# Moving a speculative check's branch and a first product, and re-dealing the splitting of weights between two engines

## The reference

```
h = W.T[x]                                  # one embedding row per token
a = layernorm(h)
s_t = tanh(A s_(t-1) + B a_t)               # a recurrence over 512 positions, s_0 = 0
o = C s
h = h + Wo (sigmoid(Wg o + bg) * o) + bo
f = layernorm(h)
e = argmax(gate_w f)                        # one of 8 experts for each token
h = h + w2[e] (silu(w1[e] f) * (w3[e] f)) + sw2 gelu(sw1 f)
```

## Time and profile before

| | |
|---|---|
| median of 3 runs | 182.56 us (180.62, 182.56, 183.18) |
| profiled execution | 182.58 us, of which the span from first to last instruction 180.7 us |
| mean granted TensorE clock | 0.971 of 2.4 GHz |
| busy: PE, DVE, ACT, POOL | 77%, 70%, 58%, 47% of the span |
| steps 15 to 53 of the recurrence | about 33 to 70 us from the span's start |
| pipeline over pairs, choice of experts | 70 to 99 us |
| gathers and blocks of tokens | 99 to 181 us |

### The profile page before, as it was taken

The page is one execution under the profiler, slowest core; times in us unless marked ns, Lnnn a source line. Parts: engine busy times, 40 slices in busy tenths (PEclk is TensorE's granted clock), DMA queues, the critical chain, the costliest instruction groups (busy, mean ns, idle before and its releaser), DMA issues.

```text
span 180.7 us, 3231 instructions
## 1 busy us (share of the span) xinstructions
PE 138.5 (77%) x997; PEld 99.7 (55%) x997; DVE 127.2 (70%) x365; ACT 104.7 (58%) x239; POOL 84.1 (47%) x77
## 2 busy tenths in 40 slices
PE   0105997788898888886799988899939989999720
PEld 0104864666675666675445878466726657666510
DVE  1245676927499995999779899488825778887730
ACT  2001444589989983587779993675532645655400
POOL 3768874900000000343100658552687787886580
PEclk9999999969999999999999999999996999999995
DMA  4564345899000000012200033410122443433331
GB/s 153 150 184 138 97 140 195 278 384 365 7 0 0 4 0 4 2 60 95 79 4 0 29 91 114 134 32 16 47 45 31 45 42 33 44 33 34 29 33 15
DMA packets 9955, 14.37 MB, mean 80 GB/s; under 512 B 1936, under 2 KB 4624, under 8 KB 9936
## 3 DMA queue, kind: packets, MB, share of 16 engines
q1 hardware_dynamic: 5904, 10.45, 16.9%
q0 software_dynamic: 4032, 3.67, 13.3%
HBM read 10.71 MB, written 3.41 MB: 78 GB/s over the span
## 4 chain that ended last, share of the span: by engine, by line
DMA 22%; PE 20%; POOL 18%; DVE 14%; ACT 12%; issue 10%; POOLq 1%; SPq 1%; DVEq 0%
DMA w_sb<-x_rows,row_in 7%; PE bank L655 6%; POOL w_sb L415 6%; POOL emb_rows L371 5%; DMA emb_rows<-emb,tok_sb 5%; POOL out L422 4%; PE bank L680 4%; DMA xblk<-x_rows,row_in 4%; ACT attn_out L725 4%; DMA w_sb<-w 3%; ACT states L702 3%; ACT w_hl L742 3%; PE bank L478 2%; PE bank L668 2%; DMA out<-w_sb,row_of 2%
## 5 line engine op out<-in xcount | busy, mean ns | idle before, releaser
L422 POOL DMA_INDIRECT out<-w_sb,row_of x20 | 31.3, 1564 | 9.1 <-DVE w_sb L1205 4.8
L478 PE MATMUL bank<-states,sq_sb 128*128 128x128 f32 x108 | 27.1, 335 | 6.0 <-ACT states L702 1.6
L655 PE MATMUL bank<-w_hl,xblk_t 128*128 x120 | 30.4, 391 | 1.0 <-issue 1.0
L403 POOL TENSOR_TENSOR rstd<-vareps,cst 128x2 f32<-128x2 f32 x8 | 5.7, 710 | 45.7 <-DVE vareps L853 45.7
L478 PEld LDWEIGHTS bank<-states,sq_sb 128*128 128x128 f32 x108 | 17.4, 202 | 14.2 <-ACT states L702 13.8
L812 ACT ACTIVATE w_sb<-bank,factor 128x512 f32<-128x512 f32 x20 | 13.8, 688 | 19.4 <-PE bank L655 19.3
L476 PE MATMUL bank<-x_in,sq_sb 128*128 128x128 f32 x108 | 23.3, 299 | 1.6 <-ACT x_in L695 1.5
L415 POOL DMA_INDIRECT w_sb<-x_rows,row_in x16 | 17.5, 1094 | 12.4 <-issue 6.3
L702 ACT ACTIVATE states<-bank 128x128 f32<-128x128 f32 x54 | 14.9, 276 | 12.2 <-PE bank L478 12.0
L680 PE MATMUL bank<-w_hl,w_sb 128*128 x160 | 16.6, 246 | 5.7 <-DVE w_sb L1205 5.7
L476 PEld LDWEIGHTS bank<-x_in,sq_sb 128*128 128x128 f32 x108 | 17.9, 207 | 2.8 <-ACT x_in L695 1.6
(11 more groups left out here) (160 smaller groups left out, 288.9 us busy)
## 6 DMA issues: line engine op xcount, KB each, us to landing
w_sb<-w SPq DMA_DIRECT2D x24, 256.0 KB, 6.4
x_rows<-norm SPq DMA_DIRECT2D x4, 256.0 KB, 2.4
out<-attn_out SPq DMA_DIRECT2D x4, 256.0 KB, 3.1
late<-places SPq DMA_DIRECT2D x1, 619.5 KB, 8.3
sw_sb<-sw SPq DMA_DIRECT2D x2, 256.0 KB, 3.0
cst<-consts SPq DMA_DIRECT2D x1, 420.0 KB, 3.3
sq_sb<-sq SPq DMA_DIRECT2D x1, 384.0 KB, 3.7
out<-w_sb,row_of POOLq DMA_INDIRECT x20, 3.3
```

Source lines behind the costliest of these rows:

```text
L422: pool.indirect_dma_start(out=out, out_offset=bass.IndirectOffsetOnAxis(ap=row_of[:, k:k + 1], axis=0), in_=out_blk[k % RING], in_offset=N ...
L478: pe.matmul(pre, at, states[:, i * COLS:(i + 1) * COLS], start=False, stop=True).then_inc(pre_ready, 1)
L655: mm = pe.matmul(hb[:], xblk_t[:, k % 3, b * P:(b + 1) * P], w[:, bass.ds(e * INNER + a * EXPERTS * INNER, INNER)], start=(j == 0), stop=( ...
```

## The change

(1) `gate(0)` goes from behind step 51 to behind step 49, and the product with C of pair 0 from behind the branch to behind step 50, into bank 6 in place of bank 0. (2) The branch comes behind step 51 in place of step 52, with `gate(1)` ahead of it; steps 52 and 53 both come behind the branch. VectorE's `gated` of pair 0 waits for a new semaphore that TensorE raises behind the branch. (3) The first three experts' low halves of w1 are written ahead of the wait for the squares, in one instruction; the fourth takes the place of the third between the two waits for TensorE. (4) The four last high halves of w2 are written by VectorE in one instruction, not by ScalarE behind steps 48 to 51, and their low halves in one instruction. (5) Ahead of the comparison VectorE does the eight low halves of w3, the wide one of w2 (experts 4 to 7) and two single ones (0 and 1); the two others (2 and 3) are one instruction behind `agree_i`, and nothing stands between the comparison and `agree_i`.

```diff
+BRANCH_STEP = STEPS - 3
+LATE_LOWS = 2
+OWN_HIGHS = EXPERTS // 2
+        c_bank = lambda n: bank[6 if n == 0 else n % 2]
...
@@ TensorE @@
-            for i in range(STEPS - 1):
+            for i in range(BRANCH_STEP + 1):
                 advance(i)
...
-                if i == STEPS - 3:
+                if i == BRANCH_STEP - 2:
+                    pe.wait_ge(wgc_ready, 1)
+                    gate(0)
+                if i == BRANCH_STEP - 1:
+                    pe.matmul(c_bank(0)[:, 0:PC], ct, kept(0), start=True, stop=True).then_inc(c_done, 1)
+                if i == BRANCH_STEP:
                     pe.wait_ge(close_ready, 1)
                     pe.transpose(bank[7][0:1, 0:P], close_row[:, 0:1], ident).then_inc(close_turned, 1)
-                    pe.wait_ge(wgc_ready, 1)
-                    gate(0)
-                if i == STEPS - 2:
                     gate(1)
                     pe.wait_ge(agree_ready, 1)
                     ok = pe.value_load(agree_i[0:1, 0:1], min_val=0, max_val=1)
...
+            pe.sem_inc(agreed, 1)
+            for i in range(BRANCH_STEP + 1, STEPS - 1):
+                advance(i)
             pe.wait_ge(state_ready, STEPS)
...
-                    if n >= 2:
+                    if n >= 3:
                         pe.wait_ge(gated_ready, n - 1)
-                    pe.matmul(bank[n % 2][:, 0:PC], ct, kept(n), start=True, stop=True).then_inc(c_done, 1)
+                    if n >= 1:
+                        pe.matmul(c_bank(n)[:, 0:PC], ct, kept(n), start=True, stop=True).then_inc(c_done, 1)
@@ ScalarE @@
-            for i in range(STEPS - 1):
+            for i in range(BRANCH_STEP + 1):
...
-                if 0 <= j < 2 * EXPERTS:
+                if 0 <= j < 2 * EXPERTS - OWN_HIGHS:
...
-                if i == STEPS - 2:
+                if i == BRANCH_STEP:
                     act.wait_ge(bg_ready, 1)
                     gate(0)
                     gate(1)
...
-            advance(STEPS - 1)
+            for i in range(BRANCH_STEP + 1, STEPS):
+                advance(i)
@@ VectorE @@
-            dve.tensor_scalar(w1_hl[:, 0, 0:half_w1], w1_sb[:, 0:half_w1], scale_of(W1), None, ALU.mult)
+            dve.tensor_scalar(w1_hl[:, 0, 0:half_w1], w1_sb[:, 0:half_w1], scale_of(W1), None, ALU.mult
+                              ).then_inc(first_high, 1)
+            dve.wait_ge(first_high, 1)
+            w1_low(slice(0, 3 * INNER))
             dve.wait_ge(squared, 2 * PARTS)
...
-            w1_low(slice(0, 2 * INNER))
             turned_greatest(1, 2)
-            w1_low(slice(2 * INNER, 3 * INNER))
+            w1_low(slice(3 * INNER, 4 * INNER))
             powers_of_two(1, SECOND)
...
-            w1_low(slice(3 * INNER, 8 * INNER)).then_inc(w_split, 1)
+            w1_low(slice(4 * INNER, 8 * INNER)).then_inc(w_split, 1)
+            own = slice(EXPERTS - OWN_HIGHS, EXPERTS)
...
+            dve.tensor_scalar(w2_hl[:, own_chunks, 0, :], by_chunk(w2_sb[:, own_cols]), scale_of(W2), None, ALU.mult
+                              ).then_inc(own_high, 1)
...
             for j in range(EXPERTS):
-                w3_low(j)
-            for j in range(EXPERTS - 3):
-                w2_low(j)
+                ins = w3_low(j)
+            ins.then_inc(w_split, 1)
+            dve.wait_ge(own_high, 1)
+            w2_low(own.start, own.stop)
+            for j in range(own.start - LATE_LOWS):
+                dve.wait_ge(w_high, EXPERTS + j + 1)
+                w2_low(j, j + 1)
...
-            w2_low(EXPERTS - 3)
             dve.wait_ge(close_turned, 1)
             dve.tensor_reduce(agree_i[:], bank[7][0:1, 0:P], AX.X, ALU.min).then_inc(agree_ready, 1)
-            w2_low(EXPERTS - 2)
-            w2_low(EXPERTS - 1)
-
+            dve.wait_ge(w_high, EXPERTS + own.start)
+            w2_low(own.start - LATE_LOWS, own.start).then_inc(w_split, 1)
...
+                    if n == 0:
+                        dve.wait_ge(agreed, 1)
...
-                                             in1=bank[n % 2][:, 0:PC], op0=ALU.add, op1=ALU.mult).then_inc(gated_ready, 1)
+                                             in1=c_bank(n)[:, 0:PC], op0=ALU.add, op1=ALU.mult).then_inc(gated_ready, 1)
```

More of the change, by code:

```diff
@@ L276, in build @@
         seq_pre, seq_state, seq_kept = sem("seq_pre"), sem("seq_state"), sem("seq_kept")
-        seq_gate, seq_tanh = sem("seq_gate"), sem("seq_tanh")
+        seq_gate, seq_tanh, seq_c, agreed = sem("seq_gate"), sem("seq_tanh"), sem("seq_c"), sem("agreed")
+        own_high, first_high = sem("own_high"), sem("first_high")
         bg_ready, resid_ready = sem("bg_ready"), sem("resid_ready")
@@ L512, in _ @@
             with pe.If(ok == 0):
-                pe.wait_ge(state_ready, STEPS)
+                pe.wait_ge(state_ready, BRANCH_STEP + 2)
                 with pe.Fori(0, CHUNKS) as c:
@@ L523, in _ @@
                     pe.matmul(gate_bank(n)[:, 0:PC], wgc[:], kept(n), start=True, stop=True).then_inc(seq_gate, 1)
+                pe.matmul(c_bank(0)[:, 0:PC], ct, kept(0), start=True, stop=True).then_inc(seq_c, 1)
+                pe.wait_ge(seq_c, 1)
                 pe.wait_ge(seq_tanh, 2)
+            pe.sem_inc(agreed, 1)
+            for i in range(BRANCH_STEP + 1, STEPS - 1):
+                advance(i)
             pe.wait_ge(state_ready, STEPS)
@@ L965, in _, with w1_low @@
             half_w1 = EXPERTS // 2 * INNER
-            dve.tensor_scalar(w1_hl[:, 0, 0:half_w1], w1_sb[:, 0:half_w1], scale_of(W1), None, ALU.mult)
+            dve.tensor_scalar(w1_hl[:, 0, 0:half_w1], w1_sb[:, 0:half_w1], scale_of(W1), None, ALU.mult
+                              ).then_inc(first_high, 1)
+            def w1_low(cols):
+                return dve.scalar_tensor_tensor(out=w1_hl[:, 1, cols], in0=w1_sb[:, cols], scalar=scale_of(W1),
+                                                in1=w1_hl[:, 0, cols], op0=ALU.mult, op1=ALU.subtract)
+            dve.wait_ge(first_high, 1)
+            w1_low(slice(0, 3 * INNER))
             dve.wait_ge(squared, 2 * PARTS)
@@ L972, in _ @@
             dve.tensor_scalar(root, sum_bits[:], 1.0, float(ROOT_BIAS), ALU.mult, ALU.add).then_inc(max_ready, 1)
-            def w1_low(cols):
-                return dve.scalar_tensor_tensor(out=w1_hl[:, 1, cols], in0=w1_sb[:, cols], scalar=scale_of(W1),
-                                                in1=w1_hl[:, 0, cols], op0=ALU.mult, op1=ALU.subtract)
-            w1_low(slice(0, 2 * INNER))
             turned_greatest(1, 2)
-            w1_low(slice(2 * INNER, 3 * INNER))
+            w1_low(slice(3 * INNER, 4 * INNER))
             powers_of_two(1, SECOND)
@@ L996, in w3_low @@
+            own = slice(EXPERTS - OWN_HIGHS, EXPERTS)
+            own_cols = slice(own.start * INNER, own.stop * INNER)
+            own_chunks = slice(own.start * IC, own.stop * IC)
+            by_chunk = lambda ap: ap.rearrange("i (c d) -> i c d", d=P)
+            dve.tensor_scalar(w2_hl[:, own_chunks, 0, :], by_chunk(w2_sb[:, own_cols]), scale_of(W2), None, ALU.mult
+                              ).then_inc(own_high, 1)
             def w3_low(j):
                 cols = slice(j * INNER, (j + 1) * INNER)
-                low_part(w3_hl[:, 1, cols], w3_hl[:, 0, cols], w3_sb[:, cols], W3, j)
@@ L1000, in w2_low @@
[L1000 to L1003, removed]
-            for j in range(EXPERTS):
-                w3_low(j)
-            for j in range(EXPERTS - 3):
-                w2_low(j)
+                dve.wait_ge(w_high, j + 1)
+                return dve.scalar_tensor_tensor(out=w3_hl[:, 1, cols], in0=w3_sb[:, cols], scalar=scale_of(W3),
+                                                in1=w3_hl[:, 0, cols], op0=ALU.mult, op1=ALU.subtract)
@@ new lines, in w2_low @@
+            def w2_low(first, end):
+                chunks = slice(first * IC, end * IC)
+                return dve.scalar_tensor_tensor(out=w2_hl[:, chunks, 1, :], in0=by_chunk(w2_sb[:, first * INNER:end * INNER]),
+                                                scalar=scale_of(W2), in1=w2_hl[:, chunks, 0, :],
+                                                op0=ALU.mult, op1=ALU.subtract)
+            for j in range(EXPERTS):
+                ins = w3_low(j)
+            ins.then_inc(w_split, 1)
```

## The result

The changed kernel is slower: 183.86 us median of 20 runs (181.1 to 188.49) against 181.38 of 20 runs of the kernel before (180.06 to 187.25); the ratio is 1.0087, 95% interval 1.0045 to 1.0129, so 1.6 us more (0.8 to 2.3). A second comparison on another occasion gave 1.0123 (1.0061 to 1.0185). The forecast was +0.4 us and 182.9; the time lies in its range, and the difference is about four times as large as forecast. The ratio leaves out runs more than 1.5% above the fastest of their kernel (ten of the changed kernel's twenty, the profiled one of 184.75 us among them, and four of the twenty of the kernel before), which is why it is smaller than the 2.5 us between the two medians. Both kernels spread by several us from one execution to the next, so most of what follows is read inside traces, from one instruction to another.

A forecast was written before the change was run, and what follows sets the result against it. The check's chain of waits was taken to bound 64 to 74 us. The branch gives 0.24 us, the longer way behind it takes 0.65: +0.4 on 182.58 makes 183.0, median forecast 182.9, range 180.9 to 184.3.

The forecast's parts named there:

- the price of the branch: Branch with register read on TensorE: 0.80 us taken, bounds 0.42 to 1.21; first work behind it at 68.24 against 68.48.
- The comparison: Start of the check's comparison on VectorE: +0.39 us, at 65.64 in place of 65.25, since VectorE is late.
- the 0.08 of L499: TensorE's L499 in step 34 needn't wait for VectorE's L921: 0.08 us gained for later steps and powers of two.
- early low halves in the idle time: w1's low halves on VectorE ahead of the squares: 1.81 us, covered by idle time with 0.35 to spare, costing nothing.
- the high half with gaps: w2's high half of 2048 values moved to VectorE, output in pieces of 128: 1.28 us long, adding 1.20.
- 2.34 for 2048 values: VectorE's merged low half of w2 ahead of the comparison, 2048 values: 0.75 + 1536 x 1.035 ns = 2.34 us.
- rival C: VectorE's high half with gaps runs at a low half's pace, 2.26 for 1.20 us: +1.45, 184.0; chance 0.15.
- From comparison to result: From the comparison to `agree_i`: reduction starts sooner, 0.22 of the 0.39 us won back, `agree_i` at 67.44 (67.27 before).
- Behind the branch: Two steps of 1.08 us, 2.16, before the second product with C, in place of 1.51: 0.65 longer.
- D: TensorE's granted clock falls to the lower level at the waits at 66.2 and 67.6: +1 to +2.5 us; chance 0.05.
- Rival B: It works: comparison not late, or branch cheap; from no change, 182.6, to -0.4 us, 182.2; chance 0.27.
- Steps 49 and 50 and ScalarE: Products put into steps 49 and 50 delay steps 50 and 51 by 0.12 and 0.24, cost 0; ScalarE loses at most 0.2.

The follow-up runs named there:

- the version with both pairs' products ahead: Changed kernel with C products of pairs 0 and 1 ahead of the branch, again behind step 52, and step 53 behind gate(2); ratios to before 0.9841 and 0.9920.
- early low halves only: Kernel before with part 3 alone: three low halves of w1 written ahead of the wait for the squares; ratio 1.0037.
- shares only: Kernel before with VectorE's part of the change and ScalarE relieved of four high halves, TensorE unchanged; ratio 1.0036.
- filler: Changed kernel with three unused products on TensorE behind gate(1), ahead of the wait for agree_i; ratio to before 1.0065.
- The kernel with code taken out: Changed kernel without register read, branch and recomputing loop on TensorE and ScalarE, which still wait for agree_i; ratio to before 1.0109.

## Why the prediction was right in direction and short in size

The step that was mis-sized is the price of the branch: 0.80 us were put in, 1.32 were measured. The forecast had the first work behind the branch 0.24 us earlier than before, and it came 0.37 later (+16.95 for +16.58), so this term had the wrong sign. The direction came out right because the second step behind the branch and VectorE's lateness are both real. That 183.86 lies in the range is partly luck: 182.9 was built on a median of three runs, 182.56, and the median of twenty is 181.38.

**The comparison: right, but for 0.08.** The forecast of +0.39 is +0.47 from VectorE's work less the 0.08 of L499; measured +0.46. Each term held: early low halves in the idle time (1.82 for 1.81), 1.28 for the high half with gaps, 2.34 for 2048 values (L1022 in the version with both pairs' products ahead). The Trainium skill, VectorE: DVE Perf Modes, section on the TRN2 errata, with its fixed 58 cycles for each instruction, would have made it +0.68 (0.47 + 0.21), an estimate; the same section says that the 58 is too low and measures about 150 (0.16 us), nearer to the 0.13 us for each instruction saved that the rows gave. The rows were right to be taken. The same page's rule on when the double rate is taken agrees with the 1.28, and rival C is dead. The 0.08 from L499 was wrong: in the changed kernel the same product (L504) starts 0.41 behind its step's too (49.91 less 49.50), though what it needs from VectorE stands at 48.99.

```profile
49.50 0.49 PE L483 MATMUL bank<-states,sq_sb 128*128 128x128 f32 x2
...
49.91 0.38 PE L504 MATMUL bank<-max_diag,cst 2*128 2x2 f32 x2
```

For the kernel before, though, the text had the wrong engine. Its comparison waits for a low half (64.58) that starts when ScalarE's copy behind step 48 ends (64.54), and 0.53 us less work on VectorE moved nothing (early low halves only, +13.35). It is in the changed kernel that VectorE alone holds the comparison, since it runs without a pause up to it.

**From comparison to result: right** (0.22 forecast, 0.20 won back).

**The branch: the term that was mis-sized.** The text took 0.80 and counted it from `gate(1)`'s second half. Counted from the end of `agree_i` it is 1.21 and 1.20 with `gate(1)` still running (before, shares only), 1.32 with nothing running (changed), and 1.32 with three more products running (filler, L481 at 68.65 less 67.33). What TensorE has queued hardly matters. The upper end of the stated bounds (0.42 to 1.21) was the plain difference of two rows, and it was the right reading: the 0.42 of idle time was only what `gate(1)` didn't cover. That is 0.5 us of the miss. The text had named 0.4 to 0.8 between `agree_i` and L476 of step 52 as a sign of being right, and the 1.32 is outside it. The Trainium skill, Advanced Engine Details and Errata, section Control Flow Timing, has 0.11 for the compare-and-branch; the run without both puts the two together at 1.18, so by that estimate the read of the register is nearly all of it; no run here separates the two. Why it is 0.11 longer with the new order no run took apart either. Every kernel with the longer value (1.31 to 1.47) has one instruction more between the branch and the next product, `sem_inc(agreed, 1)`, and none of those with 1.20 or 1.21 has it; but in those the first work is another product too.

**Behind the branch: right.** 2.16 forecast for the two steps, 2.13 measured.

**The local sum** is then 0.26 (result) + 0.11 (branch) + 0.62 (2.13 less 1.51) = 0.99 us, measured 0.98; the forecast had 0.41 (0.17 for the result, -0.41 for the branch, 0.65 behind it). The difference is the branch, 0.52 (1.32 less 0.80), and 0.09 for the result, less 0.03 for the two steps.

**The clock: the rival that was weighed too low.** D had 0.05, on the ground that TensorE is busy around it. Its own steps gave TensorE a gap of 0.7 us ahead of the turning and of about 0.7 at the branch (68.24 less the end of `gate(1)`, 66.98 + 0.59; 1.2 in truth), and it did not set them against the kernel before, where no gap between 64 and 72 us is longer than 0.42. The clock fell in 2 of 3 traces, for 1.35 to 1.9 us, inside the +1 to +2.5 that D gave. The Trainium skill, TensorE: Matmul & The Clock Gate, part 1, says that the half clock is the default state and that activity releases it; the traces agree in kind, 0.50 and 1.00 being the two levels that the windows settle at. If half of the executions have a fall of 1.5 us, that and the 0.98 make 1.7 us, an estimate; measured are 1.6 us (0.8 to 2.3). In how many of the executions behind the 1.6 the clock fell isn't known, so this supports little. The sign that the text named for D, a clock below 1.00 between 66 and 78 us, is there in two traces of three.

**Rival B** failed on both legs: the comparison was late, and the branch dear.

**Steps 49 and 50 and ScalarE: right.** Nothing waited for the two products put in there: they made steps 50 and 51 0.13 and 0.15 us later (0.12 and 0.24 forecast), and TensorE stands idle 0.71 behind them. ScalarE's branch was never the last: its tanh of step 52 starts when TensorE's product ends.

## What to carry to other kernels

The price of a branch on a value is counted from the instruction that writes the value, not from the idle time in front of the next instruction: what is queued ahead of the read hides it, and what stands behind pays all of it. So bring work to the front of the branch until the read is filled, and leave behind it only what must be there; moving the branch one step up on a serial chain puts that step behind it. Before an engine gets work taken off another, look which of the two the next wait will end on afterwards: here it became VectorE, and of the 1.20 us put on it 0.46 reached the comparison and 0.26 its result.

## What the runs showed of the hardware that was not expected

- Register read and branch on TensorE take 1.2 to 1.3 us from the end of the writing instruction (1.46 with both pairs' products ahead; 0.14 with a plain semaphore wait at the same place), and matmuls already queued run on during it.
- Idle times of 1.2 us and more were followed by the lower clock in 3 of 6 traces, shorter ones in this place in 0 of 8. That the one brings the other isn't shown.
- The kernel with code taken out was slower, not faster: 1.1% above the kernel before though attn_out of pair 0 came 0.13 us earlier (+19.57 for +19.70). Its one trace has, far from the edit, a gap of 1.12 us on TensorE with nothing to wait for. The cause is open.
